# First attention of a four-layer graph kernel: block scores with rows placed by small transfers, the mean in the head weights, values split in halves

## The reference

```python
x_proj = jnp.einsum('bnd,hdf->bhnf', x, W)          # x: layer-normed, 8 heads of 16
e_src = jnp.einsum('bhnf,hf->bhn', x_proj, a_src)
e_dst = jnp.einsum('bhnf,hf->bhn', x_proj, a_dst)
e = jax.nn.leaky_relu(e_src[..., :, None] + e_dst[..., None, :], 0.2)
e = e + (beta * jnp.log(prior + EPS))[:, None, :, :]
e = jnp.where(adj[None, None, :, :] > 0, e, neg_inf)
attn = jax.nn.softmax(e, axis=-1)
h = jnp.einsum('bhij,bhjf->bhif', attn, x_proj)      # then heads side by side
return h @ W_out.T
```

## Time and profile before

| what | us |
|---|---|
| median of 3 runs | 1065.49 |
| lowest, highest | 1058.89, 1073.07 |
| profiled execution: span from first to last instruction | 1059.3 |
| setup, to the first instruction of the attention phase | 18.8 |
| first attention, to the first instruction of the experts phase | 18.8 to 278.8 |
| PE, DVE, ACT, POOL busy in the span | 927.0, 717.5, 661.1, 504.2 |

### The profile page before, as it was taken

The page is one execution under the profiler, slowest core; times in us unless marked ns, Lnnn a source line. Parts: engine busy times, 40 slices in busy tenths (PEclk is TensorE's granted clock), DMA queues, the critical chain, the costliest instruction groups (busy, mean ns, idle before and its releaser), DMA issues. The chain is left out here.

```text
span 1059.3 us, 25141 instructions
## 1 busy us (share of the span) xinstructions
PE 927.0 (88%) x8021; PEld 805.6 (76%) x8021; DVE 717.5 (68%) x2252; ACT 661.1 (62%) x1691; POOL 504.2 (48%) x498
## 2 busy tenths in 40 slices
PE   1799998999899999999998994798898888768997
PEld 1588887887688999999998993466565666548896
DVE  4599888988464135555554544579898888678775
ACT  4556665654544546666665662688888888867652
POOL 2566564663035564444444442576767732244340
PEclk9999998999699999999999996999999999978999
DMA  7913221211354216777676861011111100000112
GB/s 195 371 50 122 120 109 70 114 42 54 101 148 131 65 49 194 212 202 197 198 200 173 210 162 33 23 33 34 32 35 28 35 6 1 1 1 20 41 42 60
DMA packets 93007, 103.59 MB, mean 98 GB/s; under 512 B 16352, under 2 KB 69856, under 8 KB 90720
## 3 DMA queue, kind: packets, MB, share of 16 engines
q1 hardware_dynamic: 73232, 59.78, 17.3%
q10 hardware_dynamic: 11472, 25.63, 9.0%
q0 software_dynamic: 8192, 16.79, 5.5%
HBM read 52.60 MB, written 43.27 MB: 91 GB/s over the span
## 5 line engine op out<-in xcount | busy, mean ns | idle before, releaser
L1319 POOL DMA_INDIRECT slot_rows_in<-xn_all,slots x128 | 130.1, 1016 | 142.7 <-DMA slot_rows_in<-xn_all,slots 105.8
L1205 ACT ACTIVATE s_hT<-s_hp,expert 128x256 f32<-128x256 f32 x284 | 111.5, 476 | 52.4 <-PE s_hp L1196 52.4
L1218 PE MATMUL s_yp<-w_experts,s_hT 128*128 x1136 | 138.0, 275 | 0.0
L1218 PEld LDWEIGHTS s_yp<-w_experts,s_hT 128*128 128x128 f32 x1136 | 132.8, 192 | 0.0
L1226 DVE TENSOR_TENSOR xnT_all<-s_yp,expert 128x256 f32<-128x256 f32 x71 | 30.2, 425 | 117.9 <-PE s_yp L1218 114.7
L489 DVE SCALAR_TENSOR_TENSOR l_mi<-l_sbc,mT 128x512 bf16<-128x512 f32 x128 | 84.3, 668 | 4.0 <-PE l_sbc L480 3.3
L1194 PE MATMUL s_hp<-e_xh,e_wh 128*128 128x256 f32 x284 | 85.9, 303 | 0.0
L1196 PE MATMUL s_hp<-e_xh,e_wl 128*128 128x256 f32 x284 | 80.1, 282 | 0.0
L1195 PE MATMUL s_hp<-e_xl,e_wh 128*128 128x256 f32 x284 | 80.1, 282 | 0.0
L1176 ACT CAST e_wh<-expert 128x512 fp32r<-128x512 f32 x71 | 43.9, 619 | 48.8 <-issue 43.1
L1120 ACT ACTIVATE s_hT<-s_hp,b_shared 128x512 f32<-128x512 f32 x64 | 42.8, 688 | 48.4 <-PE s_hp L1091 47.2
(11 more groups left out here) (353 smaller groups left out, 2701.0 us busy)
## 6 DMA issues: line engine op xcount, KB each, us to landing
expert<-expert_rows ACTq DMA_DIRECT2D x65, 322.0 KB, 3.4
slot_rows_in<-zeros SPq DMA_DIRECT2D x9, 1024.0 KB, 12.2
xnT_all<-slot_rows_in SPq DMA_DIRECT2D x71, 128.0 KB, 3.4
slot_rows_out<-xnT_all SPq DMA_DIRECT2D x71, 128.0 KB, 2.8
slot_rows_out<-zeros SPq DMA_DIRECT2D x8, 1024.0 KB, 4.4
xn_all<-l_xr SPq DMA_DIRECT2D x16, 256.0 KB, 2.3
xnT_all<-l_rT SPq DMA_DIRECT2D x16, 256.0 KB
out_dram<-xn_all SPq DMA_DIRECT2D x16, 256.0 KB, 2.3
```

The source lines that it names most:

```text
L1205: nc.scalar.activation(hT[q % 2][:, c, :], hp[:, c, 0:TILE], ACT.Gelu, bias=wt[q][:, F + c:F + c + 1]).then_inc(s["h_ok"], 1)
L1218: ins = pe.matmul(yp[q % 2][:, h * D:(h + 1) * D], hT[q % 2][:, c, h * P:(h + 1) * P], w2, start=(c == 0 and h == 0), stop=(c == FC - 1), ...
L1319: pool.indirect_dma_start(k.rows_in, bass.IndirectOffsetOnAxis(ap=k.slots[:, c, b:b + 1], axis=0), k.xn[:, b, :], None).then_inc(scattered ...
```

## The change

- The shift of normalization goes from stage n. The kernel takes the mean out of the weights instead: setup subtracts from each column of `w_heads` its mean over the 128 features (a matmul with ones and one DVE instruction), so a constant added to a row of x has no effect. ACT normalizes by scale alone.
- The shift of stage r moves from DVE to POOL, in two steps (`neg_mean_r`, then times 1/std), at the end of POOL's slot.
- Scores: ACT copies them once in f32 (`sd`) and once rounded to bf16 (first half of `sd16`). DVE subtracts the rounded from the full (`dve_y_low`, between the first two compares of its slot). PE transposes the d scores in f32 for the maxima and `sd16` as bf16 by a matmul with a bf16 identity; a graph's 32 rows of `cc` are now s high, d high, s low, d low. ACT makes `sparts` (all rows) and `dparts` (s rows replaced by ones).
- SP places rows with eight transfers a group (`sp_y_blocks`): row h of every 16 goes from `sparts` to `blocks[:, h, :]`, which holds ones in the d rows and zeros elsewhere. Then s_i + d_j of four heads is a single matmul, K = 32, 512 columns, in place of five. The selectors go.
- DVE's third exponent and the multiplication by 0.2 go; ACT makes three exponentials with scales instead, and the upper bound of 1 for the third moves into `dve_z_post` (a scalar_tensor_tensor with min and mult).
- POOL's and ACT's splitting of the values runs in halves of two graphs. The sums of graphs 0 and 1 wait for the first half only.
- SP issues the loads of x 1 to 3 in setup. In the attention phase it issues for each slot the eight transfers, one piece of zeros (18 pieces: nine for `rows_in`, nine for `rows_out`) and the stores of group g-4.

The diff, cut to what the steps need:

```diff
+                for q in range(1, 4):
+                    sp.dma_start(k.x[:, 16 * q:16 * q + 16, :],
+                                 a["x"][16 * q:16 * q + 16].rearrange("b t d -> t b d")).then_inc(k.x_loaded[q], 16)
...
-                act.wait_ge(diag_made, 6)
-                nc.scalar.copy(k.sel_s[:], diag_s[:].unsqueeze(2).to_broadcast([P, HB, P]))
...
-                act.wait_ge(load_w, 16 * 4)
-                for q in range(1, 4):
-                    load_x(q)
...
-                dve.wait_ge(diag_made, 6)
-                dve.tensor_copy(k.sel_d[:], diag_d[:].unsqueeze(2).to_broadcast([P, HB, P]))
+                dve.wait_ge(pool_made, 2)
+                dve.tensor_copy(k.ident16[:], k.ident[:])
+                dve.tensor_reduce(d_heads[:], k.ident[:].rearrange("p (q t c) -> p t c q", t=2, c=HEADS)[:, 1],
+                                  AX.X, ALU.max).then_inc(rows_made, 1)
+                dve.wait_ge(rows_made, 1)
+                dve.tensor_reduce(k.is_d[:], d_heads[:], AX.X, ALU.max).then_inc(rows_made, 1)
+                for p in range(2):
+                    dve.tensor_copy(k.blocks[p][:], d_heads[:].unsqueeze(2).to_broadcast([P, HEADS, P]))
+                dve.wait_ge(rows_made, 2)
+                dve.tensor_scalar(k.is_s[:], k.is_d[:], -1.0, 1.0, ALU.mult, ALU.add)
...
+                dve.wait_ge(pe_t, 3)
+                chain(dve.scalar_tensor_tensor(k.w_heads[:], tr[:, 3, 0:D + 16], -1.0 / D, k.w_heads[:],
+                                               ALU.mult, ALU.add))
...
+                pe.wait_ge(dve_s, 17)
+                pe.matmul(tr[:, 3, 0:D + 16], k.ones[:], k.w_heads[:], start=True, stop=True).then_inc(pe_t, 1)
...
-            wait(act, s["shift_ok"], g + 1)
-            nc.scalar.copy(act_fence[:], shift[p][:, 0:1])
+            wait(act, s["rstd_ok"], g + 1)
+            nc.scalar.copy(act_fence[:], rstd[p][:, 0:1])
             for b in range(GB):
                 ins = nc.scalar.activation(xn[:, b:b + 1, :], k.x[:, bass.ds(g * GB + b, 1), :], ACT.Identity,
-                                           scale=rstd[p][:, b:b + 1], bias=shift[p][:, b:b + 1])
+                                           scale=rstd[p][:, b:b + 1])
...
         def act_x_scores(act, g, p):
             wait(act, s["vs_ps"], g + 1)
             wait(act, s["pk_ok"], g - 1)
-            for h in range(2):
-                both = vs[:, h, 0:320].rearrange("p (b c) -> p b c", b=2)
-                ins = nc.scalar.copy(sd[p][:, :, 2 * h:2 * h + 2, :].rearrange("p k b h -> p b k h"),
-                                     both[:, :, D:160].rearrange("p b (k h) -> p b k h", k=4))
-            ins.then_inc(s["sd_ok"], 1)
-
+            nc.scalar.copy(sd[p][:].rearrange("p k b h -> p b k h"),
+                           four[:, :, D:D + 16].rearrange("p b (k h) -> p b k h", k=2)).then_inc(s["sd_ok"], 1)
+            wait(act, s["t_ps"], g)
+            nc.scalar.copy(sd16[:, :, 0, :], four[:, :, D:D + 16]).then_inc(s["s_hi"], 1)
+
+        def act_x_values(act, g, p):
+            wait(act, s["vb_ok"], 2 * (g - 1))
+            wait(act, s["pv_ps"], (g - 1) * GB)
+            nc.scalar.copy(k.v17[p][:, :, 0:DH].rearrange("p (b h) f -> p b h f", b=GB),
+                           four[:, :, 0:D].rearrange("p b (h f) -> p b h f", h=HEADS)).then_inc(s["vs_ok"], 1)
+
+        def dve_y_low(dve, g, p):
+            wait(dve, s["sd_ok"], g + 1)
+            wait(dve, s["s_hi"], g + 1)
+            dve.tensor_tensor(sd16[:, :, 1, :].rearrange("p b (k h) -> p b k h", k=2),
+                               sd[p][:].rearrange("p k b h -> p b k h"),
+                               sd16[:, :, 0, :].rearrange("p b (k h) -> p b k h", k=2), ALU.subtract)\
+                .then_inc(s["s_lo"], 1)
 
         def pe_y_transpose(pe, g, p):
             wait(pe, s["sd_ok"], g + 1)
             wait(pe, s["pk_ok"], g)
             wait(pe, s["lg_ok"], g - 4)
-            pe.transpose(cc[:, 0:P], sd[p][:].rearrange("p k b h -> p (k b h)"), k.ident[:]).then_inc(s["t_ps"], 1)
-
-        def act_y_hi(act, g, p):
+            pe.transpose(cc[0:HB, 256:256 + P], sd[p][:, 1].rearrange("p b h -> p (b h)"), k.ident[:])
+            wait(pe, s["s_lo"], g + 1)
+            pe.matmul(cc[:, 0:P], sd16[:].rearrange("p b t c -> p (b t c)"), k.ident16[:], start=True, stop=True)\
+                .then_inc(s["t_ps"], 1)
+
+        def act_y_parts(act, g, p):
             wait(act, s["t_ps"], g + 1)
+            wait(act, s["blocks_ok"], 16 * HEADS * g)
+            nc.scalar.copy(sparts[:], cc[:, 0:P]).then_inc(s["sparts_ok"], 1)
             wait(act, s["s_ps"], (g - 1) * 2 * GB)
-            nc.scalar.copy(sparts[p][:], cc[:, 0:P]).then_inc(s["hi_ok"], 1)
+            nc.scalar.activation(dparts[p][:], cc[:, 0:P], ACT.Identity, scale=k.is_d[:], bias=k.is_s[:])\
+                .then_inc(s["dparts_ok"], 1)
+
+        def sp_y_blocks(sp, g, p):
+            wait(sp, s["sparts_ok"], g + 1)
+            wait(sp, s["s_ps"], (g - 1) * 2 * GB)
+            for h in range(HEADS):
+                sp.dma_start(k.blocks[p][h:P:16, h, :], sparts[h:P:16, :]).then_inc(s["blocks_ok"], 16)
 
...
         def dve_y_max(dve, g, p):
-            wait(dve, s["hi_ok"], g + 1)
+            wait(dve, s["dparts_ok"], g + 1)
             wait(dve, s["dm_ps"], g)
-            dve.tensor_reduce(dmax[32:64, :], cc[32:64, 0:P], AX.X, ALU.max).then_inc(s["dg_self"], 1)
-            dve.tensor_tensor(sparts[p][64:128, :], cc[64:128, 0:P], sparts[p][64:128, :], ALU.subtract)\
-                .then_inc(s["sp_ok"], 1)
+            dve.tensor_reduce(dmax[0:HB, :], cc[0:HB, 256:256 + P], AX.X, ALU.max).then_inc(s["dg_self"], 1)
             wait(dve, s["dg_self"], g + 1)
-            dve.tensor_scalar(dmdiag[32:64, :], k.diag32[32:64, :], dmax[32:64, :], None, ALU.mult)\
+            dve.tensor_scalar(dmdiag[0:HB, :], k.ident[0:HB, 0:HB], dmax[0:HB, :], None, ALU.mult)\
                 .then_inc(s["diag_ok"], 1)
 
...
-            dve.tensor_tensor(us[:], cc[:, P:P + HB], s_i, ALU.add).then_inc(s["us_self"], 1)
-            wait(dve, s["us_self"], g + 1)
-            dve.tensor_scalar(pk[p][:, 1], pk[p][:, 0], 0.2, None, ALU.mult)
-            dve.tensor_scalar(pk[p][:, 2], us[:], -0.8, 0.0, ALU.mult, ALU.min).then_inc(s["pk_ok"], 1)
+            dve.tensor_tensor(pk[p][:, 1], cc[:, P:P + HB], s_i, ALU.add).then_inc(s["pk_ok"], 1)
 
...
         def pe_z_scores(pe, g, p, b):
             if b == 0:
-                wait(pe, s["sp_ok"], g + 1)
+                wait(pe, s["blocks_ok"], 16 * HEADS * (g + 1))
+                wait(pe, s["dparts_ok"], g + 1)
+            rows = slice(32 * b, 32 * b + 32)
             for h in range(2):
                 wait(pe, s["mi_ok"], g * 2 * GB + 2 * b + h - 1)
-                c = b * HEADS + 4 * h
-                pe.matmul(sbc[:, h, :].rearrange("p (q i) -> p q i", q=4), sparts[p][:], k.sel_d[:, c:c + 4, :],
-                          start=True, stop=False, skip_group_check=True)
-                for q in range(4):
-                    ins = pe.matmul(sbc[:, h, q * P:(q + 1) * P], k.sel_s[:, c + q, :], sparts[p][:],
-                                    start=False, stop=(q == 3), skip_group_check=True)
-                ins.then_inc(s["s_ps"], 1)
+                pe.matmul(sbc[:, h, :].rearrange("p (q i) -> p q i", q=4), dparts[p][rows, :],
+                          k.blocks[p][rows, 4 * h:4 * h + 4, :], start=True, stop=True).then_inc(s["s_ps"], 1)
 
...
+            if b % 2 == 0:
+                wait(pe, s["vb_ok"], 2 * g + b // 2 + 1)
...
-        def dve_r_shift(dve, g):
-            wait(dve, s["rstd_r"], g + 1)
-            dve.scalar_tensor_tensor(shift_r[:], mv_r[:, :, 0], -1.0, rstd_r[:], ALU.mult, ALU.mult)\
-                .then_inc(s["shift_r"], 1)
+        def pool_r_shift(pool, g):
+            wait(pool, s["rstd_r"], g + 1)
+            pool.tensor_tensor(neg_mean_r[:], k.zeros[:, 0:GB], mv_r[:, :, 0], ALU.subtract).then_inc(s["neg_mean_r"], 1)
+            wait(pool, s["neg_mean_r"], g + 1)
+            pool.tensor_tensor(shift_r[:], neg_mean_r[:], rstd_r[:], ALU.mult).then_inc(s["shift_r"], 1)
 
...
+            if on["y"]:
+                dve_y_low(dve, g + 1, q)
+            if on["z"]:
                 dve_z_compare(dve, g, p, 0, 1)
...
-            if on["r"]:
-                dve_r_shift(dve, g - 2)
-            if on["n"]:
-                dve_x_shift(dve, g + 3, q)
...
             if on["y"]:
                 act_x_scores(act, g + 1, q)
-                act_y_hi(act, g + 1, q)
                 act_x_values(act, g + 1, q)
+                act_y_parts(act, g + 1, q)
             if on["l"]:
                 act_r_apply(act, g - 3)
             if on["y"]:
                 act_y_exp(act, g + 1, q)
             if on["x"]:
                 act_x_xT(act, g + 2, p)
+            if on["y"]:
+                act_y_vhi(act, g + 1, q, 0)
             if on["l"]:
                 act_l_rT(act, g - 3)
```

(41 more changed lines are left out.)

139 lines of the change are left out of this document (61 added, 78 removed).

## The result

| what | before | changed |
|---|---|---|
| median, us | 1063.83 | 1100.83 |
| lowest to highest of 4 runs | 1058.89 to 1073.07 | 1087.01 to 1108.22 |
| ratio to before, 95% interval | | 1.024 [1.013, 1.035] |
| profiled execution: span | 1059.3 | 1105.8 |
| end of the first attention | 278.8 | 312.65 |

The forecast was 1044.0 us in a range of 1031 to 1060. The kernel became slower, well outside it. The ratio uses fast executions alone, while the profiled one of the changed kernel is its longest, in the slow state. The profiles here differ by 46.5 us. Of these 33.8 lie in the attention phase, which the trace splits at the bf16 transposes of the scores (L402, which takes L406's place).

A forecast was written before the change was run, and what follows sets the result against it. It took DVE and PE as near full, with DVE shifts stalling behind POOL deciding slots. Savings of 15.0 (core stage), 5.5 (head) and 1.0 (tail), 21.5 us, took the median 1065.49 to 1044.0, range 1031 to 1060.

The forecast's parts named there:

- 2.4 us of falls: Twelve attention slots: time allowed for granted-clock falls after PE idles, against 3.5 us of falls before.
- Rival (a): Attention slots: the clock falls in most, at 1.0 us a slot, 12 us in all, giving 1054 us; chance 0.2.
- a clock below 0.9 in most slots: Attention slots: one of the signs named beforehand that would show the forecast wrong.
- core stage: Twelve slots between 64.40 and 237.83 us: 173.4 us falls to 156 plus 2.4 of clock falls, saving 15.0.
- stops deciding: Plain attention slot: shorter scores cut PE to some 11.2 of 13 us, so it no longer sets the pace.
- The loop through ACT, 13.0 us: Attention slot: DVE's statistics, ACT's queue, low parts and DVE's remaining work form a loop setting 13.0 us a slot.
- Rival (c): Attention slots: no loop, ACT comes sooner, slots of 12.4 us and fewer falls, giving 1034 us; chance 0.15.
- The stalls, -10.2: Twelve slots: DVE shifts no longer wait out POOL instructions; slots of 13.6 us save 10.2, clock falls included.
- rival (b): Attention slots: DVE's low parts wait behind POOL, slots of about 13.5 us, 6 us less saved, 1050 us; chance 0.15.
- Setup and head, -5.5: Setup to second transpose of scores: SP issues x early, setup ends near 13 us, transpose near 34; saves 5.5 us.
- Transfers hidden, rival (d): Placing transfers, eight a slot at 0.47 us, stay hidden; the rival has them end last, 1095 us, chance 0.06.
- Tail, -1.0: After the twelve slots: two slots gain 0.6 to 1 each, POOL's two-step shift costs 0.2 in three groups; saves 1.0.

The follow-up runs named there:

- a3: The changed kernel with score matmuls over all 128 rows instead of 32, adding up the scores of four graphs: median 1043.05 us, ratio 0.984 to before.
- c2: The changed kernel itself, run again unaltered on another chip: median 1092.37 us, ratio 1.037 to before.
- b1: The changed kernel with four masked score copies from ACT and 128-row score matmuls, result correct: median 1063.83 us, ratio 0.987 to before.
- c3: b4 run again on another chip: median 1040.41 us, ratio 0.986 to before.
- b2: The kernel before with only the shifts changed (mean taken out of head weights, stage r's shift on POOL): median 1073.08 us, ratio 0.995 to before.
- a4: The kernel before without its four 128-column score matmuls, leaving s_i out of the pattern: median 1044.91 us, ratio 0.986 to before.
- b4: b1 with ACT copying hT before stage n's logarithm and exponential and the first half cast: median 1063.71 us, ratio 0.987 to before.
- a and c chips: The chips of the first and third sets of follow-up runs; the kernel before took 1060.04 and 1059.91 us there.
- b runs: The second set of four follow-up runs, on one chip where the kernel before took 1076.91 us.

## Why the prediction was wrong, point by point

- **The clock: the step that failed.** "I keep 2.4 us of falls." Rival (a), which the forecast gave 0.2, named the right mechanism (falls in most slots), and its sign, a clock below 0.9 in most slots, came. But it was priced at 1.0 us a slot from a slot where the fall was short (0.89 on average) and justified by gaps; that the new matmuls use 32 rows stands in neither. Measured by the pair that differs in the rows alone: 17.03 us a slot with 32 rows, 13.42 with 128 (a3), 3.6 us each, 43 over twelve slots (41 with c2's 16.80). That is the whole miss of the core stage (+31.0 against -15.0) but for 2.6 us. The other failing argument was the one against (a): slots with PE 12.99 busy of 13.60 show no fall. They ran their scores on 128 rows; the share of busy time said nothing about a PE at 32. A smaller slip: the falls of before cost 1.0 and 2.4 us by the earlier trace rows, 3.4 and not 3.5.
- **PE "stops deciding".** Its work was sized rightly: 124.89 us in the last eleven slots of a3 (73.01 to 221.11), 11.35 each, against 11.2 forecast. At the lower level for ten of 17 us DVE waited for it.
- **The loop through ACT, 13.0 us.** Not the binding wait. DVE reached the low parts after ACT in every kernel with the clock up (between 75 and 211 us a3, b1 and c3 show no idle before L391, which is L398 in b1 and c3), and the 0.4 us of idle time there did not come. What ended last was the projection behind ACT's queue. The figure was near by luck: 13.42 in a3 with that wait, 12.83 in c3 with most of it gone. Rival (c) was right on the loop; its 12.4 us was too low.
- **The stalls, -10.2.** Right for the shifts: b2, which changes little else, took 162.9 us for the twelve slots, -10.5. But in a4 the stalls of both shifts go without touching them, so their cost is no fixed sum that adds to PE's. No DVE instruction of the changed kernel's attention is over 0.87 us. L391 takes 0.21 to 0.23 us in 14 of 16 slots: rival (b) didn't come in the steady ones. Its mechanism did in two early ones, where L391 took 0.45 and 0.43 us (at 49.20 and 64.38) beside a POOL product of 0.40 us (at 49.16 and 64.33).
- **Setup and head, -5.5.** Half right. SP's issues of x last 10.33 us and the phase starts at 15.2, not near 13; the first eight placing transfers are issued in 5.00 us, not 3.8 (0.6 each, not 0.47); scores of group 0 start at 33.88, not 31.9. The second transpose came at 34.84 in f32 and 35.40 in bf16 (forecast near 34), 4.1 to 4.6 us sooner. In the changed kernel some two slots at the lower level ate that: the clock column reads 1.00 there, but each pair of score matmuls takes 1.03 us from 33.88 to 55.35 and 0.60 only from 60.30 on, where c3's takes 0.59 from 43.27 on; c3 keeps 5.2 of it at the fourth transpose (59.22 against 64.40).
- **Transfers hidden, rival (d).** Right: about 4.9 us for eight issues in a steady slot, and no wait for them.
- **Tail, -1.0.** +2.4 in the changed kernel, at a clock of 0.72 against 0.79 before; -0.1 in c3, at 0.82.

The forecast's difference for the attention phase, -21.5 us, is thus near what b4 and c3 reach (-22.8 and -24.8), which use all rows and copy hT in time. The stalls and, in part, the setup were rightly reasoned; that the slots come near 13.0 is in part luck, since the wait that gave this figure binds in neither. What stays open is why the unchanged 780 us behind the attention vary: 772 to 781 us in the profiles of the a and c chips and of before, 795 to 804 on the chip of the b runs, 793 in the first profile of the changed kernel. Between chips this is seen, and not explained.

## What to carry to other kernels

Before a matmul is cut to fewer rows to save work, ask what it does to the granted clock: a PE that looks busy can run at 1.2 GHz, and a forecast should then price a slot with most of its PE work at that level (ten of 17 us here), not by a slot with a short fall. If the operand can be masked to zero and kept at 128 rows for some spare ACT time, that costs PE nothing: the matmul took 0.38 us with 128 rows and 0.39 with 32. And when the engine that decided is relieved, look for the next wait in the in-order queue of the engine that feeds it: moving one copy ahead of three instructions was worth 0.8 us a slot here, while the new scores on full rows, without that, were worth hardly anything beside the shifts (13.67 and, without masks, 13.42 against 13.58).
